# Grouped-query and windowed attention: earlier scales and keys, a product for a copy, other banks for three outputs, another order on VectorE and ScalarE

## What is computed

```python
x = x + _L0_attn_ref(_layernorm(x), ...)            # 1 RWKV
x = x + _L0_xattn_ref(_layernorm(x), ctx, ctx)      # 2 grouped-query attention
x = x + _L0_ffn_ref(_layernorm(x), ...)             # 3 dense and expert feed-forward
x = x + _L1_attn_ref(_layernorm(x), ...)            # 4 windowed attention
x = x + _L1_xattn_ref(_layernorm(x), ctx, ...)      # 5 cross attention
x = x + _L1_ffn_ref(_layernorm(x), ...)             # 6 feed-forward

# 2: 32 query heads of 8, 8 key heads (keys and values are ctx itself)
scores = einsum('bkgsd,bktd->bkgst', qh, kh) / sqrt(8)
out = einsum('bkgst,bktd->bkgsd', softmax(scores), vh)

# 4: 16 heads of 128, 4 key heads, window 64
q = _rms_norm(x @ Wq.T, qn_w); k = _rms_norm(x @ Wk.T, kn_w)
q = q * cos + rotate_half(q) * sin; k = k * cos + rotate_half(k) * sin
att = softmax(where(mask, q k / sqrt(128), min))
out = (att v) @ Wo.T
```

## Time and profile before

| | us |
|---|---|
| median of 3 runs | 1420.6 (1420.59 to 1421.44) |
| the profiled execution | 1428.85 |
| its span | 1427.0 |
| second stage in it, about | 136.8 to 309.1 |
| windowed attention in it, about | 588 to 1073 |

### The profile page before, as it was taken

One profiled execution on the slowest core, in us unless ns is written; L12 is line 12 of the kernel. 1 busy time (PEld: TensorE's weight loads), 2 busy tenths in 40 slices (PEclk: granted clock), 3 DMA queues, 4 the chain that ended last, 5 costly groups with the idle time before them and its releaser, 6 DMA issues. The chain is left out here.

```text
span 1427.0 us, 24807 instructions
## 1 busy us (share of the span) xinstructions
PE 1228.8 (86%) x7726; PEld 944.8 (66%) x7726; DVE 965.2 (68%) x1864; ACT 760.5 (53%) x1755; POOL 605.0 (42%) x738
## 2 busy tenths in 40 slices
PE   6895899979988976389998999899987899969998
PEld 5673444448878865267776777777764565548887
DVE  5998799845755347877777777777764666643443
ACT  5432577753545455456666666666643555533332
POOL 2001555463055444576667666666653333320000
PEclk9997899968999997599999999999997999979999
DMA  9001000010025314200000000000000000000000
GB/s 326 1 0 48 19 16 16 9 60 1 5 85 156 100 51 167 107 0 1 2 0 0 0 0 0 0 0 0 1 1 4 5 3 3 3 1 1 15 15 31
DMA packets 27422, 44.74 MB, mean 31 GB/s; under 512 B 5648, under 2 KB 22160, under 8 KB 25936
## 3 DMA queue, kind: packets, MB, share of 16 engines
q1 hardware_dynamic: 23888, 34.31, 7.0%
q0 software_dynamic: 3456, 9.44, 2.5%
HBM read 32.21 MB, written 9.44 MB: 29 GB/s over the span
## 5 line engine op out<-in xcount | busy, mean ns | idle before, releaser
L2287 ACT ACTIVATE wi_weights<-wi_psum,wi_bias,wi_scale 128x128 f32<-128x128 f32 x256 | 113.9, 454 | 119.3 <-DVE wi_bias L2397 119.3
L2062 POOL TENSOR_TENSOR wi_straight<-wi_straight,wi_crossed 128x512 f32<-128x512 f32 x80 | 103.5, 1294 | 10.9 <-DVE wi_crossed L2383 10.8
L950 DVE TENSOR_REDUCE gq_least<-gq_psum 128x4 f32<-128x512 f32 x128 | 84.6, 686 | 15.9 <-PE gq_psum L843 14.2
L2050 POOL TENSOR_TENSOR wi_scratch<-wi_sums,wi_eps 128x4 f32<-128x4 f32 x80 | 35.3, 441 | 130.6 <-DVE wi_sums L2366 129.2
L2051 POOL TENSOR_TENSOR wi_scale<-wi_scratch,minus_half 128x4 f32<-128x4 f32 x80 | 84.6, 1058 | 6.3
L2388 DVE TENSOR_REDUCE wi_top<-wi_psum 128x4 f32<-128x512 f32 x64 | 44.0, 687 | 62.5 <-PE wi_psum L2177 62.5
L2186 PE MATMUL wi_psum<-wi_weights_t,wi_values 128*128 128x512 f32 x128 | 67.9, 612 | 20.5 <-DVE wi_weights_t L2404 20.5
L916 ACT ACTIVATE gq_weights_t<-gq_psum 128x512 f32<-128x512 f32 x128 | 67.6, 600 | 28.0 <-PE gq_psum L863 28.0
L2813 DVE TENSOR_REDUCE cr_top<-cr_psum 128x4 f32<-128x512 f32 x64 | 43.7, 682 | 46.2 <-PE cr_psum L2628 46.2
L2072 POOL TENSOR_TENSOR wi_weights<-wi_weights,wi_inverse 128x512 f32<-128x512 f32 x64 | 66.4, 1038 | 9.5 <-remote 5.1
L2177 PEld LDWEIGHTS wi_psum<-wi_k_t,wi_q_t 128*128 128x128 f32 x512 | 68.4, 194 | 1.7
(11 more groups left out here) (413 smaller groups left out, 3797.1 us busy)
## 6 DMA issues: line engine op xcount, KB each, us to landing
slot_y<-ex_s_out SPq DMA_DIRECT2D x20, 256.0 KB
x<-in_x_dram SPq DMA_DIRECT2D x4, 512.0 KB, 7.6
gate<-in_gate_dram SPq DMA_DIRECT2D x2, 1024.0 KB, 6.1
up<-in_up_dram SPq DMA_DIRECT2D x2, 1024.0 KB, 8.1
down<-in_down_dram SPq DMA_DIRECT2D x2, 1024.0 KB, 10.4
egu<-in_egu_dram SPq DMA_DIRECT2D x1, 2048.0 KB, 14.7
gq_keys_diagonal<-gq_key_parts SPq DMA_DIRECT2D x64, 32.0 KB, 1.9
wo<-in_wo_dram SPq DMA_DIRECT2D x1, 2048.0 KB, 8.9
```

The lines of the kernel that those rows point to most:

```text
L950: dve.tensor_reduce(least[:, n // 2 % 2, n % 2, j, :], ps[:, j % 2, :].rearrange("p (v t) -> p v t", t=P), AX.X, ALU.min).then_inc(topped, 1)
L2062: added_up = pool.tensor_tensor(straight[:, at], straight[:, at], crossed[:, at], ALU.add)
L2287: act.activation(weights[:, g % 2, j, :], ps[:, SC + g % 2, j * P:j * P + P], ACT.Exp, bias=bias[:, g % 2, j:j + 1], scale=scale[:, g, j:j ...
```

## The change

1. First stage: after `add(0)` DVE also aggregates the statistics of the first four sequences, and POOL takes their four scales. POOL splits the keys of sequences 0 to 3 there, not of 0 alone, and SP sets the diagonals of sequences 0 and 1.
2. Second stage, start: DVE normalises sequences 0 to 2 at once, sums `chosen`, then aggregates the other 12; POOL splits three sequences and then takes 12 scales. Two tables are made by ACT: the zeros of `least_parts` (POOL before) and `minus` (DVE before), ahead of ACT's first copy of the stage.
3. Second stage, each sequence: L958's copy becomes a product with ones.
4. Second stage, POOL: the eight instructions of `fold_ffn0` go one by one into iterations 4 to 11.
5. Second stage, end: `attend(29)` and `attend(30)` write banks 0 and 1, which the scores no longer use, and the turn of outputs 28 to 31 comes one half later on PE.
6. Fourth stage: in unit 3, ACT copies turned keys and queries ahead of the attended output; DVE's crossed products of the next sequence's first queries come after `take_weights(t, 2)` and no longer ahead of it.

```diff
@@ rwkv, sync and gpsimd
-            sp.wait_ge(net.keys_split, 1)
+            sp.wait_ge(net.keys_split, 4)
             sp.wait_ge(net.zeroed, 1)
-            set_keys(sp, net, 0)
+            for t in range(2):
+                set_keys(sp, net, t)
...
-            split_keys(pool, Own(pool, net.own_keys), net, 0)
+            keys_own = Own(pool, net.own_keys)
+            split_keys(pool, keys_own, net, 0)
+            pool.wait_ge(net.keys_in[1], 16)
+            for t in range(1, 4):
+                split_keys(pool, keys_own, net, t)
+            pool.wait_ge(normed, 1)
+            scale_of(pool, own, net, scratch, first_aggregated, first_rstd, 0, GB, float(HD))
@@ rwkv, vector
+            def measure_first():
+
+                own.wait()
+                dve.wait_ge(shift_ready, 1)
+                for b in range(GB):
+                    dve.bn_aggr(net.mean_var[:, b, :], net.stats[:, b, :]).then_inc(first_aggregated, 1)
...
                 if not first and not last:
                     add(g - 1)
+                    if g == 1:
+                        measure_first()
@@ gqa, gpsimd
-            scale_of(pool, own, net, scratch, aggregated, rstd_ready, 0, 1, WIDEN)
-            split_h(0)
-            scale_of(pool, own, net, scratch, aggregated, rstd_ready, 1, NB, WIDEN)
-            pool.memset(least_parts[:].bitcast(F32), 0.0).then_inc(ones_set, 1)
-            pool.wait_ge(net.keys_in[1], 16)
-            next_keys(1)
-            split_h(1)
-            next_keys(2)
-            split_h(2)
+            for t in range(3):
+                split_h(t)
+            pool.wait_ge(aggregated, NB - GB)
+            inverse_root(pool, own, net.rstd[:, GB:NB], net.mean_var[:, GB:NB, 1], scratch[:, GB:NB], WIDEN,
+                         WIDEN * LN_EPS, net.half[:, GB:NB]).then_inc(rstd_ready, 1)
...
-                if t in (NB - 3, NB - 2):
-                    fold_ffn0(pool, net, t - NB + 3)
+                if FOLD <= t < FOLD + 8:
+                    fold_ffn0(pool, net, t - FOLD)
@@ gqa, tensor
+        def out_bank(n):
+
+            return {HALVES - 3: 0, HALVES - 2: 1}.get(n, O)
...
-                need(pe, out_read, n)
+                if out_bank(n) == O:
+                    need(pe, out_read, min(n, HALVES - 3))
+                else:
+                    pe.wait_ge(topped, 4 * HALVES)
...
-                if n >= 1:
+                if 1 <= n <= HALVES - 4:
                     turn_out(n - 1)
+                elif n >= HALVES - 2:
+                    turn_out(n - 2)
+            turn_out(HALVES - 1)
@@ gqa, scalar
+            zero = net.ones[:, 0:1].broadcast_to([P, 2 * BANK])
+            act.activation(least_parts.rearrange("p s j t -> p (s j t)"), zero, ACT.Copy, scale=0.0).then_inc(tables_set, 1)
+            act.wait_ge(chosen_set, 1)
+            act.activation(minus[:], wide(chosen[:], [P, 2, P]), ACT.Copy, scale=-1.0).then_inc(tables_set, 1)
@@ gqa, vector
-                dve.tensor_copy(parts[:, :, :, :, 0], least[:, t % 2]).then_inc(least_high, 1)
+                dve.tensor_tensor(parts[:, :, :, :, 0], least[:, t % 2],
+                                  net.ones[:, 0:KV_HEADS * 4].rearrange("p (c j v) -> p c j v", c=2, j=4),
+                                  ALU.mult).then_inc(least_high, 1)
@@ windowed, scalar
                     weigh(t, g)
+                    if g == 3 and not last:
+                        take_turned("k", t + 1, 1 - s)
+                        take_turned("q", t + 1, 1 - s, 0)
                     if g > 0 or not first:
                         pt, _, pg = earlier(t, s, g, 1, U)
                         take_attended(pt, pg)
                     if g < 3:
                         take_turned("q", t, s, g + 1)
-                    elif not last:
-                        take_turned("k", t + 1, 1 - s)
-                        take_turned("q", t + 1, 1 - s, 0)
@@ windowed, vector (rotate is split into rotate and rotate_crossed)
                     if g == 3:
                         take_weights(t, 2)
+                        if not last:
+                            rotate_crossed("q", t + 1, 1 - s, 0)
```

75 lines of the change are left out of this document (40 added, 35 removed).

## The result

The changed kernel takes 1406.0 us (median of 4 runs, 1404.7 to 1406.9), the kernel before 1420.8: a ratio of 0.989, 95% interval 0.988 to 0.991. The gain is 14.8 us; 21.1 were predicted, in a range of 1390 to 1411 us. The measured time lies inside the range, but 6.5 us above the forecast itself (1399.5): it is nearer to rival C (1408.5) and to rival D (1403.5).

The account below looks back on a forecast made before the run. The second stage's steady part was taken as bound by PE, its end by a chain; terms -1.8 + 0 + 0.2 - 3.2 - 7.3 - 9.0 = -21.1 us took the 1420.6 us median to 1399.5, range 1390 to 1411.

Parts of the forecast that it names:

- rival C: Windowed attention: POOL replaces DVE as limit, its scale search pushed by the whole rotation; term 0, 1408.5 us; chance 0.13.
- rival D: Second stage's last halves: the clock falls there too, 4 us come back, 1403.5 us; chance 0.11.
- The first stage: Four more aggregations on DVE, their input wait, and a DVE product shut out by POOL's key splits: +0.9 us.
- the start: Start of second stage: first minimum 2.65 us earlier, since sequences 0 to 2 are normalised with scales that exist.
- the folds: POOL's multiplications in second stage: +0.2 us in their new places, -3.2 us in half 27 for leaving the old.
- the last halves: End of second stage: from shifted scores to last statistics 15.0 us instead of 22.3, so -7.3 us.
- The product for the copy: Second stage, each sequence: the product is shut out by POOL as the copy was, so 0 us.
- Windowed attention: Fourth stage: PE's wait for turned weights goes, each of 15 turns 0.6 us shorter, -9.0 us.
- The signs that the prediction named for it: Windowed attention: PE's weights wait gone, queries wait halved, a small new wait at L2142, a sequence 0.6 us shorter.
- E: Windowed attention: DVE's next token normalisation misses its turn and waits for POOL's join; slower, 1427.1 us; chance 0.03.
- The clock: Last halves: clock stays up, PE's longest wait being some 0.6 us, where it fell after 2.29 us.
- The distance of the profiled execution: Profiled execution before lay 8.2 us above the median of the runs, and this distance was expected to stay.

Follow-up runs that it names:

- Experiments 8 to 10: Changed kernel with, in turn: scales, keys and tables as before (1409.6 us); folds back in iterations 13 and 14 (1410.9); all outputs in bank 7, turned in own half (1408.6).
- experiment 6: Changed kernel with the second stage's product with ones made a copy again, all else as changed: 1407.0 us.
- Experiment 5: Changed kernel with DVE's second-stage normalisation of the sequence ahead moved behind the split of the minima: 1417.8 us.
- Experiment 9: Changed kernel with POOL's eight fold multiplications back in iterations 13 and 14 of the second stage, four in each: 1410.9 us.
- Experiment 7: Changed kernel with 12 spare matmuls on PE at the end of the second stage, written to banks nobody reads: 1403.8 us.
- experiment 11: Changed kernel plus later DVE normalisation with earlier POOL addition, 12 spare matmuls, and in windowed attention earlier maximum, bias and weight normalisation, ACT's old order: 1389.9 us.

## Why the prediction was right, and where it was not

**The first stage, the start, the folds and the last halves** came out as worked out, each within 0.2 us: +0.98 for +0.9, -2.70 for -2.65, -3.31 for -3.2, -7.32 for -7.3. For the first stage that is partly luck, since its length scatters by 1.7 us between executions of the same instructions. The others rest on steps that the traces after show one by one: the split ends at 140.83 (139.9 + 0.98 expected), the third normalisation gets in behind POOL's next instruction (140.86, 1.13 us long), half 27 lost the 1.92 us of the shut-out rest, and the last halves took 14.98 us for the 15.0 added up. Every later trace with these parts repeats the last two numbers to 0.03 us. Experiments 8 to 10 confirm the places, though the medians of 8 and 10 lie within the scatter.

**The product for the copy**: predicted 0, and 0 it is (experiment 6). Experiment 5 shows that the reason is the right one, 0.21 us without POOL in flight. The Trainium skill's rule ("SBUF — State Buffer", Who interferes with whom), by which a DVE instruction with two SBUF inputs blocks on a GpSimd instruction that reads SBUF, agrees with 1.13 against 0.21. The copy, with its one input in SBUF, took as long (1.12), so this pair does not single out the second input.

**Windowed attention** is the step that failed: -9.0 predicted, as 0.6 us at each of 15 turns; measured -3.4, of which the turns gave 1.1 and the end of the stage 2.3, which the prediction did not have. The signs that the prediction named for it did not come either: PE's wait for the queries was not halved, none appeared at the turn of the weights, and a sequence was 0.08 us shorter, not 0.6. Two steps of its chain broke. First "DVE's maximum moves from 722.0 to 721.4, so ACT's exponentials move from 722.91 to 722.31": the maximum moved, the exponentials did not, since the bias between them was left out of the sum. It is a product of two SBUF tensors of 4 columns. Before, it started 0.1 us ahead of the join's end (721.56 + 1.26 = 722.82) and took 0.16, to 722.87; moved 0.6 us earlier, it waits for that end. The rule for this stood at the head of the prediction and was applied to the products and copies, not to the one of 0.16 us. By that rule and the prediction's own "POOL's join behind them does not move" (it ends at 722.82) the right term could have been had: the exponentials can't start ahead of 722.82, and they already started at 722.91. Second, the sum followed what the ACT edit brought forward, the queries, and not what it pushed back, the attended output: DVE's subtraction and, behind it in DVE's order, the tokens' normalisation and the next maximum. The rival for it was E, at the right place (the normalisation of the tokens) but by another mechanism. C, with 0 for the term, came nearer to the size, but from a wrong cause: POOL's weights are ready at 726.59 on the old scale, before PE wants them; what holds PE is the turned queries, 19.5 us in all.

**The clock** was placed wrongly. The prediction took it that a wait of 2.29 us had brought it down and that with shorter waits nothing would be lost; rival D had it fall inside the last halves for 4 us. It did stay up there, but then fell at the change of stage behind them, in PE's 4.15 us without work, and the third stage's start paid 3.4 us (4.0 up to where both kernels are at full clock again). The prediction had put everything behind the second stage but windowed attention at nothing, without a reason. Experiment 9 shows that the inference was too strong: the same wait of 2.29 us does not bring it down by itself. Experiment 7 shows that the place is right: with PE at work in the gap the stretch is 4.8 us shorter.

**The distance of the profiled execution** from the median was expected to stay, 8.2 us; it went: the profiled execution of after lies at its median. The forecast was made against the median by taking it off, so this cost nothing: the sum was of differences, and all lay outside the stretch to which the 8 us are put down.

**What made up the sum**: 6.3 us less gain than forecast. 5.6 are windowed attention, 3.4 the third stage's start; against them stand 2.0 from the prologue and 0.8 in the last two stages. The 2.0 are chance, and the 0.8 lie within what other traces scatter (345.4 to 346.3 us for these stages). The 1.6 us in the last sequence of windowed attention do come with the edit, but not by the step that the prediction gave. So the total was nearer than its terms, and that it fell into the range is in part luck. What remains open is why the clock rises or falls where it does from one execution to the next.

## What to carry to other kernels

When an instruction moves in time, list every later instruction up to the one that the path needs, the smallest too, and ask of each what the engine that can shut it out has in flight then: here a bias of 0.16 us became 0.72 at one place and 0.75 at the next, and took back what PE had won. An order on three engines that is tuned to the tenth may give little for one edit; follow the wait that takes its place and make the next edit there: the later steps were worth 1.1 us a sequence where the first was worth 0.08. When a period is read from a trace, look at the stage's end too: here it held two thirds of the gain. And look at PE's clock behind a stage, not only in it, since a shorter chain can hand an idle PE to the next one.

## What the runs showed of the hardware

- What POOL shuts out on DVE goes by the operands, not by the size. A scalar_tensor_tensor of two SBUF tensors of 4 columns and a product of 32 wait for POOL's instruction to its end (0.72 and 1.13 us instead of 0.16 and 0.21), and so does the copy of 32 columns from SBUF to SBUF (1.12 in experiment 6). DVE's copy of 128x512 from PSUM beside POOL's L2090 keeps its 0.68 us, and the sum over columns of an SBUF tensor its 0.68 (719.16 in experiment 11, with POOL's join from 719.32 on). The Trainium skill ("SBUF — State Buffer", Who interferes with whom) says that a reduction never contends, which agrees; that an instruction of one SBUF input does so only in its faster modes is not told apart here, though normalisations of 128x256 took 0.41 us alone and 1.13 (140.86) behind POOL.
- The length of one wait does not tell whether the clock falls: in experiment 9 it fell behind 1.65 us and stayed at 1.0 behind 2.29, in the kernel before it was at 0.50 behind 2.29 us. It can also fall with PE at work: in experiment 7 at 302 us, during the router's products of 8 columns, PE having been busy since 295.6 but for 0.1 us.
